# One message per chunk in a two-layer graph network: the first layer computes 196 messages in place of 220

## The reference, cut to what matters

```python
h = jnp.maximum(_layernorm(x, axis=-1), 0.0)
ei = jnp.concatenate([x[src], edge_attr], axis=-1)      # x is h here
core = jnp.maximum(ei @ W1 + b1, 0.0) @ W2 + b2
gate = jax.nn.sigmoid(ei @ Wg + bg)
msg = gate * core
agg = jax.ops.segment_sum(msg, dst, num_segments=x.shape[0])
out = layernorm(agg + x) * gamma + beta
x = x + out
```

## Time and profile before

| | us |
|---|---|
| three runs | 1782.49, 1784.93, 1786.08 (median 1784.93) |
| profiled execution, its own time | 1783.17 |
| its span, first to last instruction | 1781.4 |
| edge loop, first transpose of gathered rows to last addition into `hs` | 102.7 to 902.1 |

### The profile page before, as it was taken

The page is one execution under the profiler, slowest core; times in us unless marked ns, Lnnn a source line. Parts: engine busy times, 40 slices in busy tenths (PEclk is TensorE's granted clock), DMA queues, the critical chain, the costliest instruction groups (busy, mean ns, idle before and its releaser), DMA issues. The chain is left out here.

```text
span 1781.4 us, 44262 instructions
## 1 busy us (share of the span) xinstructions
PE 1552.5 (87%) x11207; PEld 1433.5 (80%) x11207; DVE 1586.7 (89%) x3436; ACT 1243.2 (70%) x2988; POOL 1069.4 (60%) x1081
## 2 busy tenths in 40 slices
PE   6979999999999999999718689998999899898843
PEld 3779999999999999999617567777787777787633
DVE  5569999999999999999987579999999999999777
ACT  1568888888888888888545457777776767676614
POOL 0056666666666666666663177777777777777164
PEclk9989999999999999999868899999999999999877
DMA  4466666666666666666303497777777787877523
GB/s 129 161 190 186 185 186 184 188 185 185 181 189 187 185 185 187 184 187 185 104 28 149 171 290 228 231 228 224 228 229 233 217 231 223 230 223 228 193 60 102
DMA packets 165705, 333.98 MB, mean 187 GB/s; under 512 B 31015, under 2 KB 101384, under 8 KB 165092
## 3 DMA queue, kind: packets, MB, share of 16 engines
q0 software_dynamic: 70400, 231.64, 44.6%
q1 hardware_dynamic: 95204, 101.16, 17.8%
HBM read 307.63 MB, written 25.06 MB: 187 GB/s over the span
## 5 line engine op out<-in xcount | busy, mean ns | idle before, releaser
L458 POOL DMA_INDIRECT gath<-edge_in_tab,idx x440 | 464.1, 1055 | 300.6 <-DVE gate_in L882 229.1
L1147 PE MATMUL bank<-weighted,hot 128*128 128x260 f32 x880 | 237.4, 394 | 34.1 <-ACT hot L704 32.7
L1147 PE MATMUL bank<-w_lo,relu_hi 128*128 128x256 f32 x880 | 249.4, 283 | 0.0
L1147 PE MATMUL bank<-w_hi,relu_lo 128*128 128x256 f32 x880 | 249.3, 283 | 0.0
L1147 PE MATMUL bank<-w_hi,relu_hi 128*128 128x256 f32 x880 | 249.2, 283 | 0.0
L609 ACT ACTIVATE relu_hi<-bank 128x512 fp32r<-128x512 f32 x220 | 131.7, 598 | 141.5 <-PE bank L1147 141.5
L471 POOL DMA_INDIRECT kept_more<-kv_tab,idx x176 | 189.8, 1078 | 62.5 <-issue 40.2
L1147 PEld LDWEIGHTS bank<-weighted,hot 128*128 128x128 f32 x880 | 152.5, 192 | 56.3 <-ACT hot L704 41.2
L1150 PE MATMUL bank<-ident,gath 128*128 128x128 f32 x880 | 168.7, 273 | 23.7 <-DVE ea_parts L869 13.3
L891 DVE TENSOR_TENSOR msg<-bank,gate 128x512 f32<-128x512 f32 x220 | 152.2, 692 | 33.6 <-PE bank L1147 17.4
L471 POOL DMA_INDIRECT xs<-kv_tab,idx x132 | 141.6, 1073 | 52.4 <-issue 24.9
(11 more groups left out here) (269 smaller groups left out, 5054.4 us busy)
## 6 DMA issues: line engine op xcount, KB each, us to landing
ea_in<-in_ea SPq DMA_DIRECT2D x440, 64.0 KB
block_row<-row_tab SPq DMA_DIRECT2D x440, 64.0 KB
gath<-edge_in_tab,idx POOLq DMA_INDIRECT x440
kv_tab<-qkv_row SPq DMA_DIRECT2D x26, 258.0 KB, 2.4
edge_in_tab<-node_row SPq DMA_DIRECT2D x26, 256.0 KB, 2.0
xs<-in_x SPq DMA_DIRECT2D x1, 3328.0 KB, 15.0
rows_tab<-xs SPq DMA_DIRECT2D x1, 3328.0 KB, 9.3
rows_tab<-hs SPq DMA_DIRECT2D x1, 3328.0 KB, 10.9
```

The source lines that it names most:

```text
L458: g.indirect_dma_start(gath[:, q, i, :], None, edge_in_tab, bass.IndirectOffsetOnAxis(ap=idx[:, half, q, i:i + 1], axis=0)).then_inc(gath_ ...
L1147: return nc.tensor.matmul(out_, lhsT=lhs, rhs=rhs, start=start, stop=stop)
```

## The change

**One message per chunk.** `edge_inputs`, `core`, `split_edges`, `relu_inner`, `gates`, `low_edges`, `low_relu`, `add_gate`, `message`, the attribute loads and the gathers go through the 196 chunks in order. The message of chunk c goes to slot c mod 32 of a ring `msg` (32 x 512 numbers a partition, before 2 x 512). Block b picks its message from the ring by a register: ACT in `high_message` and DVE in `low_message` now load `slot_i` first. The ring lies on memory that the tables used before, so DVE waits at the loop's start for the transfers that read it. The source columns of each chunk (`src_chunk`) come from four more small products in the tables' stage and one more DVE copy.

**The last 24 blocks.** At block 196 all messages exist. For blocks 196 to 219 DVE makes the one-hot matrix by two comparisons (`hot_late`) and PE sums with two full fp32 products straight from the ring. ACT and POOL have no part in it, and `low_message` ends before it loads a register. PE loads `slot_i` itself for each of these blocks.

**Written-out programs.** SP, ACT, DVE and PE have no hardware loop in the first layer any more (`chunks_and_blocks`); POOL keeps its own.

**Beta.** The single addition becomes 26 additions of one window each (128 x 256), ahead of the gathers, each after `h_done` of its window, so during the node projection.

```diff
+MSGS = 32
+LATE = WINDOWS - 1
...
-            msg = sb(l0, "msg", [P, 2, 2 * HID], f32)
...
+            hot_late = sb(l0, "hot_late", [P, 2, 2, P], f32)
...
+            msg = sb(l0, "msg", [P, MSGS, 2 * HID], f32)
...
+        def chunks_and_blocks(engine, stages):
+            for u in range(max(count + lag for _, lag, count in stages)):
+                for stage, lag, count in stages:
+                    if 0 <= u - lag < count:
+                        stage(u - lag)
...
-                c = sp.value_load(chunk_i[0:1, ds(b, 1)], min_val=0, max_val=CHUNKS - 1)
...
-                    g.tensor_copy(idx[:, half, :, :], src_col[:, ds(b, SLOTS), :]).then_inc(idx_done, 1)
+                    g.tensor_copy(idx[:, half, :, :], src_chunk[:, ds(b, SLOTS), :]).then_inc(idx_done, 1)
...
+            pool.wait_ge(lw_in, 3 * 16)
+            for w in range(WPAD):
+                pool.wait_ge(h_done, w + 1)
+                g.tensor_tensor(xs[:, w, :], xs[:, w, :], ln0_sb[:, 1, :], ALU.add).then_inc(beta_added, 1)
...
-            g.tensor_tensor(xs[:], xs[:], ln0_sb[:, 1:2, :].to_broadcast([P, WPAD, HID]), ALU.add).then_inc(beta_added, 1)
...
-            pool.wait_ge(beta_added, 1)
+            pool.wait_ge(beta_added, WPAD)
...
+            def high_message(b):
+                m = act.value_load(slot_i[0:1, ds(b, 1)], min_val=0, max_val=MSGS - 1)
                 act.wait_ge(msg_done, b + 1)
                 after(act, sum_ready, b - 1)
-                s.copy(msg_hi[:, q % 2, :, :].rearrange("p i f -> p (i f)"), msg[:, q % 2, :]).then_inc(msg_hi_done, 1)
+                s.copy(msg_hi[:, b % 2, :, :].rearrange("p i f -> p (i f)"), msg[:, ds(m, 1), :].rearrange("p o f -> p (o f)")).then_inc(msg_hi_done, 1)
...
-            pipeline(act, [(split_edges, 0), (one_hot, 4), (distances, 3), (relu_inner, 2), (high_message, 4), (gates, 3)], BLOCKS, SLOTS)
+            chunks_and_blocks(act, [(split_edges, 0, CHUNKS), (one_hot, 4, CHUNKS), (distances, 3, CHUNKS), (relu_inner, 2, CHUNKS),
+                                    (high_message, 4, CHUNKS), (gates, 3, CHUNKS)])
...
-            v.tensor_scalar(chunk_i[:], bank[0][0:1, 0:BLOCKS], float(CHUNKS - 1), None, ALU.min)
+            step(v.tensor_scalar(slot_i[:], bank[0][0:1, 0:BLOCKS], float(CHUNKS - 1), None, ALU.min))
+            v.tensor_scalar(slot_i[:], slot_i[:], MSGS - 1, None, ALU.bitwise_and)
...
+            v.tensor_copy(src_chunk[:].rearrange("p c i -> p i c"), bank[6][:, 0:2 * CHUNKS].rearrange("p (i c) -> p i c", i=2))
...
+            def message(c):
+                dve.wait_ge(core_ready, c + 1)
+                dve.wait_ge(gate_done, c + 1)
+                after(dve, msg_lo_done, c - MSGS + LATE + 1)
+                v.tensor_tensor(msg[:, c % MSGS, :], bank[4 + c % 2][:], gate[:, c % 2, :], ALU.mult).then_inc(msg_done, 1)
+            def low_message(b):
+                if b >= CHUNKS:
+                    for i in range(2):
+                        last = v.tensor_scalar(hot_late[:, b % 2, i, :], iota_node[:], rel_col[:, b, i:i + 1], None, ALU.is_equal)
+                    last.then_inc(hot_late_done, 1)
+                    return
+                m = dve.value_load(slot_i[0:1, ds(b, 1)], min_val=0, max_val=MSGS - 1)
                 dve.wait_ge(msg_hi_done, b + 1)
-                v.tensor_tensor(msg_lo[:, q % 2, :, :].rearrange("p i f -> p (i f)"), msg[:, q % 2, :],
-                                msg_hi[:, q % 2, :, :].rearrange("p i f -> p (i f)"), ALU.subtract).then_inc(msg_lo_done, 1)
+                v.tensor_tensor(msg_lo[:, b % 2, :, :].rearrange("p i f -> p (i f)"), msg[:, ds(m, 1), :].rearrange("p o f -> p (o f)"),
+                                msg_hi[:, b % 2, :, :].rearrange("p i f -> p (i f)"), ALU.subtract).then_inc(msg_lo_done, 1)
+            def add_sums(b):
                 w = dve.value_load(win_i[0:1, ds(b, 1)], min_val=0, max_val=WINDOWS - 1)
                 dve.wait_ge(sum_ready, b + 1)
                 after(dve, sum_added, b)
                 rows = hs[:, ds(w, 1), :].rearrange("p o f -> p (o f)")
-                v.tensor_tensor(rows, rows, bank[6 + q % 2][:, 0:HID], ALU.add).then_inc(sum_added, 1)
-            pipeline(dve, [(message, 3), (low_relu, 2), (add_gate, 2), (low_edges, 0), (low_message, 3), (add_sums, 4)],
-                     BLOCKS, SLOTS)
+                v.tensor_tensor(rows, rows, bank[6 + b % 2][:, 0:HID], ALU.add).then_inc(sum_added, 1)
+            dve.wait_ge(steps_out, 2 * HEADS * 16)
+            dve.wait_ge(row_out, 32)
+            chunks_and_blocks(dve, [(message, 3, CHUNKS), (low_relu, 2, CHUNKS), (add_gate, 2, CHUNKS), (low_edges, 0, CHUNKS),
+                                    (low_message, 3, BLOCKS), (add_sums, 4, BLOCKS)])
...
+            for i in range(2):
+                for c in range(2):
+                    at = i * CHUNKS + c * HALF_C
+                    mm(bank[6][:, at:at + HALF_C], nat_f[:, 0, c, i * P:(i + 1) * P], ident[0:HALF_C, 0:HALF_C], True, True)
...
+            def sum_messages(b):
+                if b >= CHUNKS:
+                    m = pe.value_load(slot_i[0:1, b:b + 1], min_val=0, max_val=MSGS - 1)
+                    pe.wait_ge(msg_done, CHUNKS)
+                    pe.wait_ge(hot_late_done, b - CHUNKS + 1)
+                    for i in range(2):
+                        last = mm(bank[6 + b % 2][:, 0:HID], hot_late[:, b % 2, i, :],
+                                  msg[:, ds(m, 1), i * HID:(i + 1) * HID].rearrange("p o f -> p (o f)"), i == 0, i == 1)
+                    last.then_inc(sum_ready, 1)
+                    return
...
-            pipeline(pe, [(edge_inputs, 0), (sum_messages, 3), (core, 1)], BLOCKS, SLOTS)
+            chunks_and_blocks(pe, [(edge_inputs, 0, CHUNKS), (sum_messages, 3, BLOCKS), (core, 1, CHUNKS)])
```

More of the change, by code:

```diff
@@ L40 @@
 FAR_APART = 2.0 ** 100
[L41 removed]
+assert CHUNKS % (2 * SLOTS) == SLOTS and MSGS % SLOTS == 0 and MSGS > LATE + 4 and BLOCKS % KEEP == 0 and KEEP % BROWS == 0
 def build(nc, x, src, dst, etype, ea, w1, wg, b_cat, w2, b2, ln0, query_col, wqkv, b_qkv, rel, wo, b_o, ln1, out):
@@ L81, in build @@
         rel_col = sb(ctx, "rel_col", [P, BLOCKS, 2], f32)
-        chunk_i = sb(ctx, "chunk_i", [1, BLOCKS], i32)
+        slot_i = sb(ctx, "slot_i", [1, BLOCKS], i32)
         win_i = sb(ctx, "win_i", [1, BLOCKS], i32)
@@ L597, in _ @@
             pipeline(act, [(normed(h_done), 0), (far_rows, 2), (high_rows, 1)], WPAD, 2)
-            def split_edges(k, q):
-                b = SLOTS * k + q
-                act.wait_ge(ea_arrived[q], 32 * (k + 1))
-                after(act, z_ready, b - SLOTS + 1)
-                s.copy(ea_parts[:, q, :], ea_in[:, q, :]).then_inc(ea_hi_done, 1)
-            def relu_inner(k, q):
-                b = SLOTS * k + q
-                act.wait_ge(z_ready, b + 1)
-                after(act, core_ready, b - 1)
-                s.activation(relu_hi[:, q % 2, :], bank[q % 2][:], ACT.Relu).then_inc(relu_hi_done, 1)
@@ L611, in gates, with split_edges @@
-            def gates(k, q):
-                b = SLOTS * k + q
-                act.wait_ge(gate_added, b + 1)
-                after(act, msg_done, b - 1)
-                s.activation(gate[:, q % 2, :], gate_in[:, q % 2, :], ACT.Sigmoid).then_inc(gate_done, 1)
-            def high_message(k, q):
-                b = SLOTS * k + q
+            def split_edges(c):
+                slot = c % SLOTS
+                act.wait_ge(ea_arrived[slot], 32 * (c // SLOTS + 1))
+                after(act, z_ready, c - SLOTS + 1)
+                s.copy(ea_parts[:, slot, :], ea_in[:, slot, :]).then_inc(ea_hi_done, 1)
@@ new lines, in relu_inner, with gates @@
+            def relu_inner(c):
+                act.wait_ge(z_ready, c + 1)
+                after(act, core_ready, c - 1)
+                s.activation(relu_hi[:, c % 2, :], bank[c % 2][:], ACT.Relu).then_inc(relu_hi_done, 1)
+            def gates(c):
+                act.wait_ge(gate_added, c + 1)
+                after(act, msg_done, c - 1)
+                s.activation(gate[:, c % 2, :], gate_in[:, c % 2, :], ACT.Sigmoid).then_inc(gate_done, 1)
+            def high_message(b):
+                m = act.value_load(slot_i[0:1, ds(b, 1)], min_val=0, max_val=MSGS - 1)
@@ L862, in _, with low_edges @@
             pipeline(dve, [(low_rows, 0), (add_bias, 1)], WPAD, 2)
[L865 to L867 removed]
+            def low_edges(c):
+                slot = c % SLOTS
+                dve.wait_ge(ea_hi_done, c + 1)
                 rows = slice(EDGE_DIM, 2 * EDGE_DIM)
[L869 to L875 removed]
@@ L893, in low_message, with low_relu @@
-            def low_message(k, q):
-                b = SLOTS * k + q
+                v.tensor_tensor(ea_parts[rows, slot, :], ea_in[rows, slot, :], ea_parts[rows, slot, :], ALU.subtract).then_inc(ea_lo_done, 1)
+            def low_relu(c):
+                dve.wait_ge(relu_hi_done, c + 1)
```

(2 more changed lines are left out.)

132 lines of the change are left out of this document (56 added, 76 removed).

## The result

| | before | after |
|---|---|---|
| median of four runs, us | 1784.94 (1782.49 to 1786.08) | 1720.05 (1715.71 to 1722.02) |
| profiled execution, us | 1783.17 | 1721.67 |
| its span, us | 1781.4 | 1719.9 |
| last addition into `hs`, us | 901.71 | 839.38 |

The changed kernel takes 0.9633 of the time before (95% interval 0.9615 to 0.9651), 64.9 us less. I forecast 1718 and 1704 to 1748. In the profiled executions 62.3 us are gained up to the last addition into `hs`, of 61.5 in all: the stages behind it take the same time.

What follows compares the result with a forecast made beforehand. PE was taken to bound the edge loop at 3.53 us a step. Chunks -84.7, beta -15.9, register loads 0, late blocks +31.2 and tables +2.4 gave -67.0 us: profiled 1716.2, median forecast 1718, range 1704 to 1748.

Steps and rivals of the forecast that it cites:

- The price of a step: Edge loop: PE stays the bound at 3.53 us a step, so 24 fewer steps save 84.7 us.
- The rival of a DVE that is a little late: Edge loop: DVE's register loads show 0.1 us in each of 196 steps, 20 us, giving 1738; chance 0.15.
- Beta: End of the edge loop: the single addition's stall goes, 15.9 us less; 26 pieces in the node projection cost 0.
- The register loads: Edge loop: one new load a step on DVE and on ACT costs 0, with ends 0 and 0.84 us a step.
- the load under `msg_lo`: Edge loop, DVE: the existing load between `msg_lo` and `hs` runs while queued operations execute and costs nothing.
- the slack of 0.21: Edge loop: DVE's idle time of 0.21 us a step, 44.3 us over 216 steps.
- The rival at 1841: Edge loop: DVE's new load fully exposed behind `ea_parts`, 196 x 0.63 = 123 us, slower than before; chance 0.05.
- the zero: Edge loop: the 0 us put down as the cost of the new register loads.
- The late blocks: Last 24 blocks: 1.3 us each, 31.2 us added, from DVE's 0.84 load and 0.41 addition; range 20.9 to 61.
- The rival of a lower clock: Last 24 blocks: PE at 0.50 of its clock, 31 us more, giving 1749; chance of slow late blocks 0.13.
- The tables: Ahead of the node projection: small products 1.6 us, DVE copy 0.62, `slot_i` step 0.2; 2.4 us added, bounds 0 to 4.
- The sum: Whole kernel: -84.7 - 15.9 + 0 + 31.2 + 2.4 = -67.0 us, profiled execution 1783.17 to 1716.2.

Runs made afterwards that it cites:

- e1: The kernel before with only its single beta addition replaced by the 26 early pieces; 1995.95 us against 2013.53, ratio 0.9917.
- e2: The changed kernel with beta again as one addition behind the last gather; 1949.18 us, ratio 0.9695 to the kernel before.
- e9: The changed kernel with POOL's loop over the gathers written out too; 1720.55 us against 1786.59 for the kernel before, ratio 0.9639.
- e11: The changed kernel run again unaltered, as base of the third group; 1721.71 us, ratio 0.9635 to the kernel before.
- e7: The changed kernel without DVE's new register load in the loop, low_message reading a fixed slot; 1917.23 us, ratio 0.9537 to the kernel before.
- e5: The changed kernel run again unaltered, as base of the second group; 1930.08 us against 2011.18 for the kernel before, ratio 0.9616.
- e6: The changed kernel with four buffers for the late one-hot matrices, made two blocks earlier; 1927.85 us, ratio 0.9595 to the kernel before.
- e4: The kernel before with its first-layer loops on SP, ACT, DVE and PE written out, nothing else; 1993.91 us, ratio 0.9907.
- e3: The changed kernel with beta's 26 pieces behind the last gather instead of in the node projection; 1937.78 us, ratio 0.9614.

## Why the prediction was right

**The price of a step: right.** PE's step stayed 3.53 us, and 24 fewer gave 24 x 3.53 = 84.7 us. What the step did not show is the pause. It costs PE 0.15 us each time, since DVE's slack and its faster next step take up the rest, and over the loop 196 x (3.549 - 3.534) = 2.9 us. The rival of a DVE that is a little late named 0.1 us a step; it was 0.015.

**Beta: right**, in place and size. The stall of 15.9 us is gone, e1 measured 17.6 for it alone, and e2 brought it back. The piece is 0.74 us, not 0.55: a price taken as one long instruction's share leaves out what each instruction costs by itself. It did not matter, since POOL had 46 us of room.

**The register loads: right for the step, but not free.** DVE's flat-out step of 3.31 us, with the load and without it, is the measured form of what I argued from the load under `msg_lo`. The 0.22 us between it and 3.53 are also the slack of 0.21 that I had read off. The rival at 1841 had its whole weight on this. What the zero left out is the pause. It comes before `hs` once in 8 steps with the load (e9, e11) and once in 32 without it (e7, on another chip), and e7 was 12.9 us faster than e5. On the chip of the first result all pauses together cost 2.9 us; how much of that is the load's was not measured there.

**The late blocks: size nearly right, mechanism wrong.** I put 1.3 us a block and called it DVE's own chain, 0.84 for its load and 0.41 for its addition. It was 1.18 (24 x 1.18 = 28.3 us for 31.2), and DVE's load is no part of it. I had written that DVE's comparisons "lie beside PE's products". They do for every other block only. DVE can begin the next matrix only behind an addition that waits for PE, and then PE waits for DVE: a chain that goes round both engines, though each has idle time. e6 breaks it without touching a load, and PE then runs through at 1.03. The rival of a lower clock did not occur (1.00 throughout).

**The tables: the term that was too small.** 2.4 us were put down, 3.0 is what the tables themselves took. The eight products took 2.03 us where I had worked out 1.6, and the copy 0.56. Another 3.3 came in the projection, which the prediction had left as it was. The runs say that this is mostly not the change's. The changed kernel itself had a projection of 46.1 us in its first profile, 43.3 in e5 and 43.8 in e11; the kernel before had 42.9 in its one profile. Over all kernels the length runs from 42.9 to 46.1, with the pieces of beta and without them. The half clock of 3.4 us that the first profile shows is absent from e5 and e11 and present in e4, which has no pieces there.

**The sum.** -84.7 - 15.9 + 6.3 (front) + 2.9 (pauses) + 28.3 (late blocks) = -63.1 us up to the last addition, and 62.3 were measured. The forecast's -67.0 was off by 3.9 at the front and 2.9 for the pauses, and 2.9 the other way in the late blocks. That the median came within 2.1 us is in part luck: the forecast for the profiled execution was 1716.2 and it took 1721.67, 5.5 more. I had put the median 1.8 us above the profiled execution, and it came 1.6 below.

## What to carry to other kernels

A register load that stands behind long operations in an engine's queue did not lengthen the step here, even where that engine was the bound; read its price at the engine's flat-out step, not where its queue is empty. But count the instructions it adds: pauses came more often with it. Where two engines hand short pieces to and fro and both show idle time, look for the chain round both of them: two more buffers and the producer two blocks earlier gave 0.15 us a block here, and taking PE's register load out of the chain half as much. An elementwise operation of GpSimd on SBUF belongs where VectorE reads PSUM, or must be cut into pieces as long as the wait that VectorE can bear.

## What the runs showed of the hardware

- Beside 26 GpSimd instructions of 0.7 us (e3), VectorE's operations with one PSUM input keep their duration (0.67 and 0.68 us), and those with two SBUF inputs grow by 0.4 us each. Comparisons from SBUF to SBUF with one input tensor grow as well, from 0.48 to 1.11 us for two.
- VectorE's pause of about 0.5 us comes before `hs` once in 8 steps where its traces record 16 instructions a step (e9, e11), and once in 32 where they record 12 (e7). Both fit one pause in 128 instructions.
- The same kernel before took 1786.6 us on one chip and 2011.2 and 2013.5 on two others. e1, with the same loop, has pauses in front of `hs`, put down to issue, in almost every other step there; the kernel before had none in its loop in the profile of 1783 us.
- The same program can have 3.4 us at TensorE's lower clock, 1.2 GHz, in its node projection in one profile and none in another (0.50 from 60.9 to 64.3 us in the first profile of the changed kernel; none in e5 and e11).
- PE kept its upper clock, 2.4 GHz, through the late blocks, 800 to 840 us, in which it was busy for 33.1 of 40 us.
